# Hybrid convolution, attention and expert kernel: a head's final addition moved from GpSimd to VectorE

## What is computed

```python
x = conv_attention(x)                      # 1x1 convolutions, softmax over 32 x 32 channels
t = tokens(x)                              # (16, 1024, 256)
t = t + attn(layernorm(t))                 # differential attention, below
t = t + ffn(layernorm(t))                  # shared expert + top 2 of 8 experts
# attn, for each of 8 heads of 32 channels:
a1 = softmax(q1 @ k1.T / 32 ** 0.5)        # 1024 x 1024
a2 = softmax(q2 @ k2.T / 32 ** 0.5)
o  = (a1 - lam[h] * a2) @ v                # the two halves of a head
xn = groupnorm(o, 4 groups over channels and tokens)
y  = xn @ out_w.T + out_b
```

## Time and profile before

| | us |
|---|---|
| median of 3 runs | 5967.44 (5963.66 to 5967.7) |
| the profiled execution | 5965.52 |
| its span in the trace | 5963.7 |

### The profile page before, as it was taken

One profiled execution on the slowest core, in us unless ns is written; L12 is line 12 of the kernel. 1 busy time (PEld: TensorE's weight loads), 2 busy tenths in 40 slices (PEclk: granted clock), 3 DMA queues, 4 the chain that ended last, 5 costly groups with the idle time before them and its releaser, 6 DMA issues.

```text
span 5963.7 us, 117362 instructions
## 1 busy us (share of the span) xinstructions
PE 5762.7 (97%) x39472; PEld 3674.9 (62%) x39472; DVE 5002.4 (84%) x6839; ACT 3258.7 (55%) x5868; POOL 2957.8 (50%) x1334
## 2 busy tenths in 40 slices
PE   6999999999999999999999999999999999999999
PEld 4566565655657556575665756657566575665656
DVE  5978879798897988979889798897978979788797
ACT  4645546455564655646556465564655646555464
POOL 3816538074380744708347183561825628266281
PEclk9999999999999999999999999999999999999999
DMA  2212222122222222222222221222212222122221
GB/s 78 59 48 62 60 55 54 56 58 58 53 52 62 54 58 55 49 61 58 57 55 50 63 58 55 55 51 63 60 49 56 50 63 59 49 60 50 65 59 47
DMA packets 148810, 338.00 MB, mean 57 GB/s; under 512 B 38624, under 2 KB 61280, under 8 KB 139744
## 3 DMA queue, kind: packets, MB, share of 16 engines
q1 hardware_dynamic: 146400, 329.26, 22.7%
q10 hardware_dynamic: 1792, 1.12, 0.1%
HBM read 90.49 MB, written 17.30 MB: 18 GB/s over the span
## 4 chain that ended last, share of the span: by engine, by line
PE 79%; DVE 10%; issue 6%; DMA 2%; ACT 2%; SPq 0%; DVEq 0%; ACTq 0%
PE psum L1141 18%; PE psum L1363 16%; PE psum L1285 15%; PE psum L1306 14%; PE psum L1460 7%; DVE minus_max L834 5%; PE psum L1313 4%; PE psum L1193 1%; PE psum L1332 1%; PE psum L1414 1%; PE psum L1291 1%; DMA prob_sums<-combine_rows_dram 1%; DMA stack<-stage 1%; DVE small L749 1%; DVE small L886 1%
## 5 line engine op out<-in xcount | busy, mean ns | idle before, releaser
L579 ACT ACTIVATE probs<-psum 128x512 f32<-128x512 f32 x4096 | 2215.8, 595 | 1249.8 <-PE psum L1363 1220.1
L423 POOL TENSOR_TENSOR prob_sums<-prob_sums,probs 128x1024 f32<-128x1024 f32 x960 | 2288.2, 2383 | 475.6 <-DVE prob_sums L930 396.2
L834 DVE TENSOR_REDUCE minus_max<-psum 128x1 f32<-128x1024 f32 x2048 | 2397.8, 1206 | 145.7 <-PE psum L1285 132.7
L1363 PE MATMUL psum<-stack 98*128 98x512 f32 x4096 | 1439.1, 431 | 3.5 <-DVE max_rows L844 3.5
L1285 PE MATMUL psum<-stack 96*128 96x512 f32 x4096 | 1219.4, 406 | 39.7 <-DVE minus_max L834 28.9
L1306 PE MATMUL psum<-probs,v_tokens 128*32 128x256 f32 x16384 | 1112.3, 387 | 0.0
L393 POOL TENSOR_TENSOR stage<-probs,stage 128x512 fp32r<-128x512 f32 x16 | 20.7, 1295 | 2130.9 <-ACT probs L545 2130.9
L1363 PEld LDWEIGHTS psum<-stack 98*128 98x128 f32 x4096 | 712.1, 189 | 541.4 <-ACT probs L579 331.6
L1285 PEld LDWEIGHTS psum<-stack 96*128 96x128 f32 x4096 | 713.8, 189 | 324.5 <-DVE minus_max L834 143.5
L1306 PEld LDWEIGHTS psum<-probs,v_tokens 128*32 128x32 f32 x16384 | 453.0, 110 | 468.1 <-issue 227.4
L423 POOL TENSOR_TENSOR prob_sums<-probs 128x1024 f32<-128x1024 f32 x240 | 573.9, 2391 | 273.3 <-ACT probs L579 273.3
(11 more groups left out here) (162 smaller groups left out, 5163.7 us busy)
## 6 DMA issues: line engine op xcount, KB each, us to landing
stack<-stage SPq DMA_DIRECT2D x1024, 128.0 KB, 3.0
stack<-stage SPq DMA_DIRECT2D x256, 256.0 KB, 3.1
prob_sums<-combine_rows_dram SPq DMA_DIRECT2D x128, 256.0 KB, 3.8
stage<-combine_rows_dram SPq DMA_DIRECT2D x128, 256.0 KB, 3.3
x_tile<-x_dram SPq DMA_DIRECT2D x34, 512.0 KB, 3.6
x_tile<-o_head SPq DMA_DIRECT2D x480, 32.0 KB, 1.9
y_dram<-residual SPq DMA_DIRECT2D x16, 512.0 KB, 2.8
y_dram<-stage SPq DMA_DIRECT2D x16, 512.0 KB, 2.9
```

The source lines that it names most:

```text
L423: nc.gpsimd.tensor_tensor(total, first, probs[:, k % NP, :], ALU.add).then_inc(sum_pool, 1)
L579: nc.scalar.activation(probs[:, k % NP, half * HALF:(half + 1) * HALF], ps[:, exp_bank(k) + half, :], ACT.Exp).then_inc(p_ready, 1)
L834: v.tensor_reduce(nm[:, u % 2, q:q + 1], flat_in, AX.X, ALU.max, negate=True).then_inc(ring_free, 1)
L1363: mm(ps[:, exp_bank(k) + half, :], stack[0:KS, s, 1, kt * P:(kt + 1) * P], stack[0:KS, s, 0, half * HALF:(half + 1) * HALF], start=True, s ...
```

## The change

`add_head` moves from GpSimd to VectorE, with the same operands and the same semaphores. VectorE runs it behind the maximum of kt = 1 in odd units from 3 on (head (u-3)/2). `head_statistics` moves within VectorE, from ahead of the maximum of kt = 0 to behind that of kt = 1, in even units from 4 on. GpSimd keeps nothing of a head.

```diff
# GpSimd
-                def add_head(h):
-
-                    pool.wait_ge(o_free, b * UNITS + 2 * h + 2)
-                    nc.gpsimd.tensor_tensor(oh[:, h % 2, :], oh[:, h % 2, :], ot[:, :],
-                                            ALU.add).then_inc(oh_ready, 1)
-
                 for u in range(UNITS - 1):
-                    if u % 2 and u >= 3:
-                        add_head((u - 3) // 2)
...
-                add_head(HEADS - 2)
# VectorE
+                def add_head(h):
+
+                    dve.wait_ge(o_free, b * UNITS + 2 * h + 2)
+                    v.tensor_tensor(oh[:, h % 2, :], oh[:, h % 2, :], ot[:, :], ALU.add).then_inc(oh_ready, 1)
+
                 def ahead_of_score(u, kt):
 
-                    if u % 2 == 0 and u >= 4 and kt == 0:
-                        head_statistics((u - 4) // 2)
                     if u and kt == 4:
                         sum_recips(u - 1, 1)
 
                 def beside_score(u, kt):
 
+                    if u % 2 and u >= 3 and kt == 1:
+                        add_head((u - 3) // 2)
+                    if u % 2 == 0 and u >= 4 and kt == 1:
+                        head_statistics((u - 4) // 2)
                     if u and kt == 3:
                         sum_recips(u - 1, 0)
```

## The result

| | us |
|---|---|
| before, median of 4 runs | 5966.73 (5963.66 to 5967.7) |
| changed, median of 4 runs | 6093.3 (6076.3 to 6125.69) |
| ratio | 1.0219, 95% interval 1.0205 to 1.0232 |
| profiled execution of the changed kernel | 6125.69, span 6123.8 |

The change makes the kernel 2.2% slower; 6089 was forecast. The time also spreads over 49 us now, where it spread over 4, and the profiled execution is the slowest of the four. Its span is 160.1 us above that of before.

What follows compares the result with a forecast made beforehand. VectorE was taken as the bound. Per batch 5.7 (units 3, 9, 11, 13) + 1.2 (unit 5) + 1.5 (unit 7) - 0.8 (statistics) = 7.6 us, x 16 = 122; 5965.5 + 122 = 6087, 6089 with the median's offset; range 5948 to 6105.

Steps and rivals of the forecast that it cites:

- Who paces whom: Odd units: GpSimd's add_head starts its additions 0.70 us late, VectorE's pair sum stalls 0.68 us, and TensorE pays.
- The race: Units 3, 5, 9, 11, 13: VectorE's and GpSimd's additions start level; VectorE was taken to wait the whole 2.39 us.
- The bracket: Rows from unit 14: VectorE starting 0.08 us behind GpSimd loses, queued some 0.1 us before it wins.
- Price of a lost race: Unit 9, VectorE waiting for GpSimd's addition: next maximum +2.10 us, pair sum's 0.68 stall gone, net +1.42 a unit.
- Unit 5: Next maximum +2.10 us, partly taken by 0.80 us of idle before L829: about +1.2 (bounds 0 and 2.1).
- unit 7: VectorE's addition comes inside a running GpSimd addition and waits 1.6 us: +1.5 (bounds 0 and 1.7).
- Statistics: Moved head_statistics in even units: 0.2 us gained in each of units 4, 10, 12 and 14, -0.8 a batch.
- Unit 15: VectorE's addition meets a GpSimd addition, but replaces a wait of L883 or L886 and L964's for add_head: near 0.
- Rival A: VectorE starts first in units 3, 5, 9, 11, 13 and does not wait: -0.5 us a batch, 5959 us; chance 0.27.
- Rival C: Starts jitter by hundredths, so VectorE waits in only part of the level starts; half of 80 gives 6023 us; chance 0.12.

Runs made afterwards that it cites:

- one input: Changed kernel with statistics of the second half in place of VectorE's addition, those heads left unadded: 5934.97 us, ratio 0.9946 against before.
- PSUM: Changed kernel with the second half of a head written to PSUM instead of SBUF, whole computation: 5939.15 us, ratio 0.9952 against before.
- third maximum: Changed kernel with VectorE's addition behind the maximum of kt = 2 instead of kt = 1: 5997.8 us, ratio 1.0048 against before.
- GpSimd's later start: Changed kernel with a one-element GpSimd addition ahead of GpSimd's first addition in odd units from 3 on: 5979.03 us, ratio 1.0021 against before.
- VectorE later: Changed kernel with a short VectorE instruction of 8 elements ahead of its head addition: 6201.2 us, ratio 1.0386 against before.
- first maximum: Changed kernel with VectorE's addition behind the maximum of kt = 0 instead of kt = 1: 6043.48 us, ratio 1.0128 against before.

## Why the prediction was right, point by point

- *Who paces whom.* Right. GpSimd's `add_head` stalls the pair sum by 0.68 us in odd units and TensorE pays: with it gone and nothing put in its way (one input, PSUM) the pair of units 9 and 10 falls from 27.57 to between 26.9 and 27.0 us.
- *The race.* Right in kind: level within hundredths in units 3, 5, 9, 11 and 13. I took it as lost throughout, "at about even odds"; it was lost in 55 of 80. The bracket was rough: I had VectorE win at a lead of 0.05 us or more, it took 0.02. And L883, the row that tipped my choice, is a copy with one SBUF input, not an instruction with two; that it stands for the addition was not shown. That step was off by some 45 us, what 25 races would have cost more (1.6 to 1.9 us each).
- *Price of a lost race.* The addition ended 0.29 us behind GpSimd's (0.32 expected); the next maximum, counted from the unit's start, came 2.04 us later than in the kernel before (2.10). Net 1.37 to 1.39 in units 3, 9 and 11 and 1.48 in 13, with the statistics in, against 1.42 - 0.2.
- *Unit 5* +1.6 for 1.2 expected, within its bounds; *unit 7* +1.39 for 1.5, all 16 additions between 1972 and 1982 ns.
- *Statistics.* Mis-sized, about 0.1 us a unit or nothing for 0.2.
- *Unit 15.* "Near 0" holds: the wait moved as described (the addition takes 2.48 us there, L886's wait is gone), and at the same clock the stretch from unit 15 on is 0.1 to 0.2 us longer. What else it grew by is the clock. The kernel with the third maximum, where that addition takes 0.42, comes to 152.4 and 153.5 at clocks of 0.99 and 0.98, so the wait is worth 0.3 us at most.
- *What was missing.* The clock. Nothing in the prediction has TensorE's own speed fall. It cost some 65 us in the profiled execution, 55 of them behind lost races. With every race lost, the forecast of 6089 would have been 112 us short of the 6201 measured.
- *Rival A*, races won, was priced at 5959; forced by GpSimd's later start it came to 5979: a start put off brings part of the pair sum's stall back (10 of the 20 us), and the rest lies in the stretch from unit 15 on. *Rival C*, mixed races, is what happened; its 6023 lacked the clock as well.

In the profiled execution the terms add up so, in us over all batches:

| | |
|---|---|
| forecast for this execution | +122 |
| 25 races won, not lost | -45 |
| lost races, unit 5 and statistics mis-sized (8.6 a batch for 7.6) | +16 |
| the clock | +65 |
| the rest, mostly from unit 15 on | +2 |
| measured | +160 |

So for the execution that the sum was made for it was 38 us short, with errors of 45 us one way and some 80 the other. The four executions lie between 6076 and 6126, at granted clocks of 0.982 to 0.987, and their median fell 4 us from the forecast: the mechanism held, that closeness is luck. How many races the other three lost isn't known.

## What to carry to other kernels

Before an elementwise step moves to VectorE beside a busy GpSimd, count its SBUF inputs: with two, look up in the timeline what GpSimd runs at that moment and add the rest of that instruction to the price; with one in PSUM it ran free of that in all 112 cases. One SBUF input is not safe for every operation, though: the statistics in the place of the addition never waited, but L883, a `tensor_copy` of 8 elements from SBUF to SBUF, does. In the kernel before it takes 2.33 to 2.34 us in the 16 cases that start beside a GpSimd addition and 0.17 in the 16 others (shortest, median and longest):

```profile
L883 DVE COPY small<-small x32: 170/1252/2344, 315.7 to 5850.6; 128x8 f32<-128x8 f32 x32
```

So look at the duration of each kind of instruction beside GpSimd's, small ones too. Two engines that count from the same event meet at the same place every time, so a level start is no rare accident, and a start that looks like a gap in one engine's timeline may be the worst place on the other's. A stall of 1.8 us on TensorE costs more than itself where the clock falls behind it (1.5 to 4.5 us more here), so price long stalls apart from short ones.

## What the runs showed of the hardware

**Where the level race is decided.** From the starts of the two records in ns, over the 80 races of the changed kernel:

| VectorE's start ahead of GpSimd's | won | lost |
|---|---|---|
| 27 to 84 ns | 20 | 0 |
| 19 to 22 ns | 5 | 2 |
| 16 ns or less, down to 26 ns behind | 0 | 53 |

So it takes a lead of some 20 ns in the records, not a level start. The Trainium skill ("SBUF — State Buffer", "Who interferes with whom") has the first to issue hold the ports for its whole instruction; the traces agree for both engines, with 2.68 us on VectorE in a lost race and 2.63 instead of 2.39 us on GpSimd in a won one. By another page of the Trainium skill, "Perfetto Trace Analysis" ("Per-engine timelines"), as I read it, level records should have favoured VectorE. The measurement says GpSimd.

**The clock behind a stall.** Within a pair of units the granted clock of TensorE fell to 1.2 GHz in 25 of the 55 lost races and in none of the 25 won. What TensorE did before, by its longest idle piece in the pair, in the changed kernel and those with VectorE later, with the first and with the third maximum:

| idle ahead of it, us | cases | clock fell |
|---|---|---|
| none, or 0.29 (unit 13) | 25 | 0 |
| 0.61 to 0.69 (third maximum; units 3, 9, 11, 13) | 64 | 0 |
| about 1.0 (first maximum) | 80 | 2 |
| 1.17 to 1.20 (unit 7) | 32 | 1 |
| 1.48 to 1.54 (unit 5) | 26 | 0 |
| 1.75 to 1.81 (units 3, 9, 11, 13) | 109 | 74 |

The same idle time came with a fall and without (1.76 us at 1412.20 with, 1.79 us at 1032.67 without). A fall cost 1.5 us where the clock of the pair was 0.94 and 4.5 where it was 0.85. What decides among the 109 is open. The stretch from unit 15 on has such falls in every kernel, that of before too.
